# A hybrid block of four stages on one core: the last transposes of logits of stages 2 and 4, and the products that spread the choice of clusters in stage 4, stand one chunk of dense products later in TensorE's order

## What is computed

```
stage 1   y = xn @ ((w1.T @ w2.T) * sparse_mask) + b2 ; x1 = x  + gelu(y)
stage 2   ffn(xn, weight, bias, centroids)             ; x2 = x1 + ffn
stage 3   single-head attention, width 128, Wo and bo  ; x3 = x2 + attention
stage 4   the same ffn                                 ; x4 = x3 + ffn

ffn:      dots  = softmax(x @ centroids.T / 0.1)       # 64 clusters
          hits  = dots > 0.01
          query = any(hits over clusters)              # one bit a token
          chosen = any(hits over all tokens)           # one bit a cluster
          out   = where(query & chosen[assignments], x @ weight.T + bias, 0)
```

## Time and profile before

| what | value |
|---|---|
| median of 3 runs | 275.42 us (275.40 to 275.84) |
| the profiled execution | 275.24 us, of which the span from first to last instruction is 273.4 us |
| TensorE busy | 268.8 us (98%), 1397 matmuls and transposes |
| VectorE busy | 192.2 us (70%) |
| ScalarE busy | 177.0 us (65%) |
| GpSimd busy | 163.8 us (60%) |
| mean granted TensorE clock | 0.999 of full speed |
| DMA | 18.25 MB, 67 GB/s in the mean |

### The profile page before, as it was taken

How to read it: one execution, slowest core, us unless ns; L and a number is a source line. 1 busy time by engine, 2 the same in 40 slices (tenths; PEclk the granted TensorE clock), 3 DMA queues, 4 the chain that set the end, 5 groups by cost and what they waited for, 6 DMA issues and landing times.

```text
span 273.4 us, 4428 instructions
## 1 busy us (share of the span) xinstructions
PE 268.8 (98%) x1397; PEld 225.6 (82%) x1397; DVE 192.2 (70%) x406; ACT 177.0 (65%) x359; POOL 163.8 (60%) x196
## 2 busy tenths in 40 slices
PE   8999999999999999999999999999999999999995
PEld 8787888888888888788988888888888888887784
DVE  3988988605935867794478796788447584875994
ACT  3855886455477786448889988779544747577500
POOL 4883988265395491189896993990541247102795
PEclk9999999999999999999999999999999999999999
DMA  7999064800000000000000000000000000000096
GB/s 253 372 362 326 14 219 167 305 4 2 0 0 0 2 0 2 0 2 0 2 0 0 1 4 0 0 2 0 2 2 0 0 2 0 1 2 0 36 361 220
DMA packets 10247, 18.25 MB, mean 67 GB/s; under 512 B 1200, under 2 KB 1968, under 8 KB 10224
## 3 DMA queue, kind: packets, MB, share of 16 engines
q1 hardware_dynamic: 8784, 15.47, 16.2%
q10 hardware_dynamic: 1440, 2.49, 2.5%
HBM read 13.76 MB, written 4.19 MB: 66 GB/s over the span
## 4 chain that ended last, share of the span: by engine, by line
PE 96%; DMA 1%; DVE 1%; POOL 1%; issue 0%; ACT 0%; DVEq 0%; POOLq 0%
PE m_bank L1018 76%; PE t_bank L1113 12%; PE m_bank L1197 6%; PE t_bank L1119 1%; DMA x_tok<-in_L_attn_a_x 1%; PE m_bank L1073 1%; ACT xn_odd L613 0%; PE t_bank L1138 0%; DVE st L817 0%; POOL rstd L471 0%; POOL ve L470 0%; DVE y_tok L988 0%; DVE x_tok L994 0%; PE m_bank L1144 0%; PE t_bank L1124 0%
## 5 line engine op out<-in xcount | busy, mean ns | idle before, releaser
L1018 PE MATMUL m_bank<-ffn_hi,even_hi 128*128 128x512 f32 x96 | 38.9, 406 | 0.0
L1018 PE MATMUL m_bank<-ffn_lo,even_hi 128*128 128x512 f32 x96 | 37.6, 392 | 0.0
L1018 PE MATMUL m_bank<-ffn_hi,even_lo 128*128 128x512 f32 x96 | 37.4, 390 | 0.0
L602 ACT ACTIVATE ones_and_squares<-x_tok,mv 128x512 bf16<-128x512 f32 x44 | 31.6, 717 | 4.1 <-DVE x_tok L921 3.7
L559 POOL TENSOR_TENSOR y_tok<-y_tok,x_tok 128x512 f32<-128x512 f32 x12 | 15.3, 1289 | 25.6 <-ACT y_tok L755 25.6
L539 POOL TENSOR_TENSOR y_tok<-y_tok,bias_f 128x512 f32<-128x512 f32 x16 | 20.6, 1295 | 16.2 <-ACT y_tok L696 16.2
L467 POOL TENSOR_SCALAR ve<-mv 128x1 f32<-128x1 f32 (+1 forms) x20 | 5.3, 264 | 37.9 <-ACT ones_and_squares L602 36.9
L824 DVE TENSOR_TENSOR even_lo<-t_bank,even_hi 128x512 fp32r<-128x512 f32 x24 | 16.2, 684 | 12.8 <-ACT even_hi L645 12.6
L471 POOL TENSOR_TENSOR rstd<-ve,half 128x1 f32<-128x1 f32 (+1 forms) x31 | 23.5, 758 | 2.6
L824 DVE TENSOR_TENSOR odd_lo<-t_bank,odd_hi 128x512 fp32r<-128x512 f32 x28 | 18.8, 686 | 6.4 <-ACT odd_hi L645 6.2
L1018 PE MATMUL m_bank<-odd_hi,wqkv_hi 128*128 128x512 f32 (+1 forms) x60 | 21.5, 358 | 0.0
(11 more groups left out here) (191 smaller groups left out, 784.8 us busy)
## 6 DMA issues: line engine op xcount, KB each, us to landing
x_tok<-in_L_attn_a_x SPq DMA_DIRECT2D x3, 1024.0 KB, 9.8
xn_odd<-in_L_attn_a_xt SPq DMA_DIRECT2D x2, 1024.0 KB, 7.3
out<-x_tok ACTq DMA_DIRECT2D x8, 256.0 KB, 2.2
out<-x_tok SPq DMA_DIRECT2D x7, 256.0 KB, 2.2
x_tok<-in_L_attn_a_x SPq DMA_DIRECT2D x4, 256.0 KB, 4.1
w_raw<-in_L_attn_a_w SPq DMA_DIRECT2D x4, 256.0 KB, 5.0
xt_other<-in_L_ffn_weight SPq DMA_DIRECT2D x4, 256.0 KB, 5.9
y_tok<-in_L_attn_a_sparse_mask SPq DMA_DIRECT2D x4, 256.0 KB, 6.5
```

What stands on the lines that cost most here:

```text
L602: act.activation(squares, x_tok[:, n, :], ACT.Square, bias=sum_of(*key), scale=-float(D), accum_out=mv[:, i, 1:2]).then_inc(done[kind], 1)
L1018: ins = pe.matmul(bank, a, w, start=(first and n == 0), stop=(last and n == count - 1))
```

## The change

Only TensorE's order is edited, in three places.

```
@@ stage 2 @@
-dn2.3.3.c1 dn2.2.3.c21 dn2.2.0.c2 cl2.3.h0 cl2.3.h1 dn2.2.2.c3 tc.2.3 dn2.2.2.c1 dn2.2.0.c1 dn2.2.2.c2
+dn2.3.3.c1 dn2.2.3.c21 dn2.2.0.c2 cl2.3.h0 cl2.3.h1 dn2.2.2.c3 dn2.2.2.c1 tc.2.3 dn2.2.0.c1 dn2.2.2.c2
@@ stage 4 @@
-cl4.3.h0 dn4.2.1.c1 cl4.3.h1 dn4.2.1.c2 tc.4.3 dn4.2.1.c3 dn4.2.3.c1 dn4.2.1.c0 dn4.3.0.c2 dn4.2.3.c0 dn4.3.0.c0
-dn4.2.3.c3 dn4.3.0.c31 bestT.4 dn4.3.2.c2 tmask.4 masks.4 dn4.3.2.c031 dn4.2.2.c0123 dn4.3.1.c0123 dn4.2.0.c0123
+cl4.3.h0 dn4.2.1.c1 cl4.3.h1 dn4.2.1.c2 dn4.2.1.c3 tc.4.3 dn4.2.3.c1 dn4.2.1.c0 dn4.3.0.c2 dn4.2.3.c0 dn4.3.0.c0
+dn4.2.3.c3 dn4.3.0.c31 bestT.4 dn4.3.2.c20 tmask.4 masks.4 dn4.3.2.c31 dn4.2.2.c0123 dn4.3.1.c0123 dn4.2.0.c0123
```

## The result

Five runs of the changed kernel took 277.41 us in the median (276.68 to 277.74), five of the kernel before beside them 275.42 (275.30 to 275.84). The ratio is 1.0055, with a 95% interval of 1.0037 to 1.0073, or +1.0 to +2.0 us. A later group of runs gave 276.92 us (276.82 to 277.37) and 1.0047 (1.0030 to 1.0063). The forecast was 276.02 us and a range up to 276.6. The direction was right and the size was not.

A forecast was written before the change was run, and what follows sets the result against it. TensorE was taken as the bound: +0.44 us from stage 2 and +0.14 from stage 4 (0.45 - 0.31) give 0.58, plus 0.02 for the last stores. On the median 275.42 that gave 276.02 us, range 275.5 to 276.6.

The forecast's parts named there:

- What the change removes: TensorE's waits before the moved steps, 0.25, 0.24 and 0.31 us; if simply filled, TensorE would end 0.80 us earlier.
- Stage 2, +0.44: At tc.2.3, transposes start 0.44 us later, bestT.2 waits 0.76 us, and stage 4 begins 0.44 us late.
- Stage 4, `tc.4.3`: Transposes start 0.45 us later, best1.4 and the blend follow, and TensorE is 0.45 us late in this stage.
- The bank behind `bestT.4`: VectorE's blend4.2.3 frees the bank for the product after bestT.4, so that product moves from 255.40 to 255.85.
- `tmask.4` and `masks.4`, -0.31: In stage 4, the 0.31 us wait for csel.4 before the spreading products is gone, with 0.8 us of margin.
- The end: TensorE's last product and the end move by 0.58 us, plus 0.02 us for the overlapping last stores.
- the two paths: To the end: TensorE to storeh.3.3.1, landing at 273.61, and GpSimd's additions to store.2.2, landing at 273.52.
- The term for the last stores: At the end, store.2.2 and storeh.3.3.1 now overlap, priced at 0.02 us.
- the faster one: Rival: the waits of 0.80 us are simply filled, bestT.2 and bestT.4 being ready in time; 274.62 us, chance 0.08.
- The one in which only stage 2 is lost: Rival: the blend does not hold the product at 255.40, stage 4 gives -0.22 us; 275.64 us, chance 0.14.
- The collision of the last stores: Rival: store.2.2 and storeh.3.3.1 are in flight together and each pays 0.7 us; 276.70 us, chance 0.08.

The follow-up runs named there:

- The guard: The whole change, with GpSimd's addition xb.2.1 also waiting until lmax.4.3 is done; median 276.00 us, ratio 1.0018 to the kernel before.
- the maximum in PSUM: The whole change, with the maximum of the batch 3 logits in stage 4 written to a PSUM bank; ratio 1.0016 to the kernel before.
- the split chunk: Kernel before with moved tmask and masks, earlier xb.2.0, maximum in PSUM, plus one dn4.2.1.c3 product ahead of tc.4.3, two behind; ratio 0.9990 to the kernel before.

## Why the prediction was wrong

- **What the change removes**: right. The waits before the moved steps were 0.25, 0.24 and 0.31 us, and they are gone.
- **Stage 2, +0.44**: right, measured +0.40. The wait of 0.76 us worked out for `bestT.2` was 0.93 - 0.23 = 0.70. Nothing took the delay up by stage 4.
- **Stage 4, `tc.4.3`**: here it failed. The step moved the transposes by 0.45 us (measured 0.45) and then said: "The same chain takes `best1.4` from an end at 254.69 to 255.14". It took the chain's length as fixed. It grew by 0.78 us, because the addition on GpSimd, which does not wait for `tc.4.3`, now began ahead of one of its links and held it. The guard and the maximum in PSUM both take the surplus away. That the link was sensitive stood in the trace of before, in the view of the tile ncmx and in two rows of the timeline:

```profile
L937 DVE SCALAR_TENSOR_TENSOR ncmx<-cmx,rstd x8: 161/163/666, 76.9 to 250.7; 128x4 f32<-128x4 f32 x8
```

```profile
76.28 1.30 POOL L539 TENSOR_TENSOR y_tok<-y_tok,bias_f 128x512 f32<-128x512 f32 x1
...
76.93 0.67 DVE L937 SCALAR_TENSOR_TENSOR ncmx<-cmx,rstd 128x4 f32<-128x4 f32 x1
```

There are eight operations of one shape, with a median of 163 ns and one of 666. That one began inside an addition of GpSimd and ended 0.02 us after it (77.60 and 77.58). The next addition of GpSimd began 0.08 us after the start of the last of the eight. A shift of 0.45 us had to put the operation behind the addition's start.

- **The bank behind `bestT.4`**: right. The row of after names the blend again, with 0.30 us, and the split chunk bears it out.
- **`tmask.4` and `masks.4`, -0.31**: right for the move alone (0.9988), and right in the sum, but credited to the wrong edit. With `tc.4.3` moved, the blend holds the product behind `bestT.4` so long that csel is ready in time even where tmask was not moved (in the run with `tc.4.3` alone tmask follows its product by 0.23 us). So by these rows the third edit buys TensorE nothing in the whole change. No run has the first two edits without the third, but `tc.2.3` alone (+0.25 us) and `tc.4.3` alone (+1.0) already add up to the +1.3 of the whole.
- **The end**: the two paths were right, and both were late. The term for the last stores was too small. The forecast took 0.02 us and read the trace of before as showing no overlap of `store.2.2` and `storeh.3.3.1`; by its own landing times they were in flight together there from 271.33 to 272.63. In the five profiles at full clock in which the last SyncE store was issued 0.89 us or more behind ScalarE's last one, it took 1.7 us to land, and in the eight in which it followed within 0.6 us, it took 1.8 to 2.0 us. So the meeting of the stores cost some 0.1 to 0.3 us. This is a comparison of profiles; no run brought the two stores closer with all else unchanged. The Trainium skill (Trainium Kernel Development and Optimization, Key Constraints) was cited for DMAs of all queues sharing the DMA engines, and these times agree with it.
- **The rivals**: the faster one fell, with `bestT.2` waiting. The one in which only stage 2 is lost fell too, since the blend was what held the product behind `bestT.4`. The collision of the last stores came in kind, but at less than half of its price of 0.7 us, and most of the surplus came from another collision. That one has a rule: the Trainium skill (SBUF — State Buffer, Who interferes with whom and the summary behind it) says that VectorE and GpSimd share one pair of SBUF ports as a lock, that an operation of VectorE with two SBUF inputs contends for it with one of GpSimd that reads SBUF, and that the second one waits until the first has finished. The traces agree: held with two inputs from SBUF (0.98 and 0.80 us), not held with one of them in PSUM (0.16), and not held when VectorE comes first (0.16). That GpSimd waits in that last case is not visible: its addition is shown with 1.29 us either way. This collision should have been a rival, and it would have given 275.42 + 0.60 + 0.8 = 276.8, near the 276.92 of the second group and inside the interval of the first.
- **The median of the first group**, 277.41, is 0.5 us higher than that of the second. In its profiled execution the opening was 0.87 us late, ahead of all edits. The other four have no profile, so for them this is not shown.

## What to carry to other kernels

Where engines run fixed orders, a move does not only shift a chain, it shifts it against everything on the other engines that keeps its own time. Before pricing a shift, look for the work on GpSimd that starts within the shift's length of each VectorE operation of the chain, and look at the maximum of each group's durations beside its median: an outlier can be a collision that has already happened once, and the timeline around it tells. And fill a wait only if what stands behind the moved step has slack; a wait in front of a chain that TensorE itself will wait for is not idle time to be had.

## What the runs showed of the hardware

- A VectorE operation of 128x4 with two inputs from SBUF took 0.16 us alone and 0.98, 0.98 and 0.80 us when it started 0.34, 0.34 and 0.51 us into a GpSimd addition of 1.29 us. It ended 0.02 to 0.03 us after the addition. With one of its inputs in PSUM it took 0.16 us in the same place.
- Of operations with one input from SBUF, some were held and some were not. The reduction of line 935 took its 0.42 us although it started 0.06 us into an addition (the run that moved only ScalarE's `qb` steps). In the trace of before, an operation of line 946 took 0.63 us, where the median is 0.17, and ended 0.03 us after an addition that had begun before it; the reciprocal of line 945, inside the same addition, took 0.18 us.

```profile
101.20 1.29 POOL L539 TENSOR_TENSOR y_tok<-y_tok,bias_f 128x512 f32<-128x512 f32 x1
```

```profile
101.67 0.18 DVE L945 RECIPROCAL crec<-csum 128x4 f32<-128x4 f32 x1
101.89 0.63 DVE L946 TENSOR_SCALAR qsel<-crec 128x4 f32<-128x4 f32 x1
```

- The store of 128 KB that ends the kernel took 1.7 us to land when it was issued 0.89 us or more behind the last one of the other queue, and 1.8 to 2.0 us when it followed within 0.6 us.
- The opening of one and the same kernel was 0.87 us late in one profiled execution and 0.13 us in another.
